# Packing the last tokens of eight experts four to a tile: 34 expert tiles for 39, first weights streamed

## The reference, cut to what matters

```python
xn = layernorm(x)
# attention branch, per token t and head (4 heads of 64)
y_t[i] = sum_j r_t[j] * (S[i,j] + u[j]*k_t[j]*v_t[i]);  S[i,j] = S[i,j]*exp(w_t[j]) + k_t[j]*v_t[i]
attn = (groupnorm(y) * gamma + beta) * g @ Wo.T
# expert branch
probs    = softmax(tokens @ Wr + br)            # 4096 x 8
expert   = argmax(probs);  max_prob = probs[expert]
h        = relu(tokens @ W1[expert] + b1[expert])   # 256 -> 512
ffn      = (h @ W2[expert] + b2[expert]) * max_prob # 512 -> 256
out = x + attn + ffn
```

## Time and profile before

| | |
|---|---|
| median of 3 runs | 571.99 us (569.68 to 573.77) |
| the profiled execution | 572.14 us, span 570.9 us, mean granted TensorE clock 0.988 |
| PE busy | 525.3 us (92% of the span) |
| DVE busy | 440.6 us (77%) |
| ACT busy | 334.5 us (59%) |
| POOL busy | 196.2 us (34%) |
| DMA | 64.03 MB, mean 112 GB/s |
| HBM | read 42.92 MB, written 24.12 MB |

### The profile page before, as it was taken

The page is one execution under the profiler, slowest core; times in us unless marked ns, Lnnn a source line. Parts: engine busy times, 40 slices in busy tenths (PEclk is TensorE's granted clock), DMA queues, the critical chain, the costliest instruction groups (busy, mean ns, idle before and its releaser), DMA issues. The chain is left out here.

```text
span 570.9 us, 20266 instructions
## 1 busy us (share of the span) xinstructions
PE 525.3 (92%) x7946; PEld 465.4 (82%) x7946; DVE 440.6 (77%) x1104; ACT 334.5 (59%) x756; POOL 196.2 (34%) x156
## 2 busy tenths in 40 slices
PE   2889798888999999999999999989999999999984
PEld 2668687776898899989899899979998989989873
DVE  6877899988867696868778886949686877878552
ACT  4964656225574756566665657565655656575751
POOL 7901010121324434334344232533442533523332
PEclk9999999898999999999999999999999999999998
DMA  8978662699431534434333434243443433332334
GB/s 284 305 272 274 183 168 62 158 363 319 108 61 30 111 54 91 75 84 74 90 56 79 78 67 77 49 94 53 95 71 84 70 92 56 66 46 49 48 44 46
DMA packets 57633, 64.03 MB, mean 112 GB/s; under 512 B 10706, under 2 KB 51923, under 8 KB 57395
## 3 DMA queue, kind: packets, MB, share of 16 engines
q1 hardware_dynamic: 44578, 47.77, 29.7%
q0 software_dynamic: 11840, 14.42, 17.3%
q10 hardware_dynamic: 1120, 0.54, 0.3%
HBM read 42.92 MB, written 24.12 MB: 117 GB/s over the span
## 5 line engine op out<-in xcount | busy, mean ns | idle before, releaser
L1802 POOL DMA_INDIRECT out<-rows,dst_row x39 | 64.5, 1654 | 210.1 <-DVE rows L1192 184.7
L704 PE MATMUL F<-xsT,w1s 128*128 128x128 f32 x624 | 76.9, 276 | 2.8 <-issue 1.7
L1064 DVE SCALAR_TENSOR_TENSOR mix<-G,vec,ba 128x256 f32<-128x256 f32 x160 | 69.7, 477 | 12.6 <-PE G L474 12.5
L704 PEld LDWEIGHTS F<-xsT,w1s 128*128 128x128 f32 x624 | 74.6, 192 | 5.5 <-issue 2.5
L712 PE MATMUL F<-w,hsT 128*128 x312 | 74.9, 383 | 0.3 <-ACT hsT L1596 0.3
L1596 ACT ACTIVATE hsT<-F,b1c 128x128 f32<-128x128 f32 x156 | 44.5, 368 | 34.9 <-PE F L704 31.0
L712 PEld LDWEIGHTS F<-w,hsT 128*128 128x128 f32 x312 | 57.2, 190 | 8.5 <-issue 0.5
L1103 DVE COPY_PREDICATED AP_<-msk,LL 128x256 f32<-128x256 uint32 x96 | 51.1, 532 | 16.4 <-issue 11.1
L1125 DVE TENSOR_TENSOR RK<-RK,D 128x256 f32<-128x256 f32 x112 | 47.3, 423 | 19.3 <-issue 11.0
L1072 DVE TENSOR_TENSOR mix<-mix,xnT 128x512 f32<-128x512 f32 x80 | 55.1, 689 | 1.6
L1788 POOL DMA_INDIRECT rows<-xn_d,src_row x39 | 41.0, 1050 | 31.9 <-PE F L693 14.4
(11 more groups left out here) (192 smaller groups left out, 1195.4 us busy)
## 6 DMA issues: line engine op xcount, KB each, us to landing
cd<-cd_d SPq DMA_DIRECT2D x30, 320.0 KB, 5.8
w<-in_W SPq DMA_DIRECT2D x16, 512.0 KB
cd_d<-w SPq DMA_DIRECT2D x32, 160.0 KB, 2.7
b2t<-in_b SPq DMA_DIRECT2D x38, 128.0 KB
w<-in_x SPq DMA_DIRECT2D x8, 512.0 KB, 9.0
xn_d<-w SPq DMA_DIRECT2D x8, 512.0 KB
out<-in_x SPq DMA_DIRECT2D x8, 512.0 KB, 5.4
out<-res POOLq DMA_DIRECT2D x16, 256.0 KB, 4.6
```

Of the source, the lines that this page charges most:

```text
L704: i1 = pe.matmul(FB[:, k * P:(k + 1) * P], w1s[:, cc, k, :], xsT[:, cc, :], start=(cc == 0), stop=(cc == 1))
L1064: i1 = dve.scalar_tensor_tensor(mixed_in(u, c, n, cc), bk[:, cc * UN:(cc + 1) * UN], cvec(LAM + CC * n, cc), ba[:, cc, :, :].rearrange("p ...
L1802: pool.indirect_dma_start(io["out"], bass.IndirectOffsetOnAxis(dst_row[:, f:f + 1], 0), ys[:, f % 2, :], None, compute_op=ALU.add).then_in ...
```

## The change

Tiles are now of two kinds. 25 full tiles hold 128 tokens of one expert each. What is left over of the experts is cut into quarters of 32 tokens, each of one expert, and four quarters make one of 9 quad tiles: 34 tiles for 39. The quads are `fa` of halves 2 to 6 and `fc` of halves 8 to 11. Halves 7 to 13 are now all short (two tiles).

- Full tile: the first weights come from memory by `first_weights` (512 KB) into one of two buffers; ACT's copy `weights` is gone. The rest is as before.
- Quad tile: `hidden` is turned round. The stationary operand is 32 tokens, the moving one 512 columns of the quarter's own W1, and each quarter has its own group of 32 columns of PE (`tile_position=(0, 32*t)`). DVE then adds `b1` (`biased`, 128x512), PE transposes the sum with 4 transposes (`turned`), ACT rectifies with one instruction of 512 columns, and `down` runs 16 matmuls of 256 columns in the four column groups. `quarters` loads four W1, three W2 (the first quarter uses the resident W2) and four `b1` per quad, 11 DMAs; `bias` is four DMAs of 32 partitions.
- W1 is no longer resident; its place holds the quads' weights. W2's load now stands without W1's ahead of it, and the first `first_weights` and `quarters(0)` follow when the experts of the tiles are known (`ex`).
- The routing has 28 numbered steps instead of 16. `tiles_of_experts` is 16 small instructions instead of 5, `places` 4 instead of 1, `experts_of_tiles` 4 instead of 3.
- `rectified(fa)` on ACT stands behind `squares`. For a quad `fc`, `rectified` stands behind `block` and `gated_back`.
- `first_bias`, the gathers, the row sums and all attention code are unchanged; the mask table is stored more tightly.

```diff
-FT = (TOK + E * (P - 1)) // P
-EACH = [0 if h == 0 else 2 if h % 6 == 1 else 3 for h in range(NU - 2)]
+QR = P // 4
+FULL = -(-(TOK - E * (P - 1)) // P)
+QUADS = -(-((TOK - FULL * P + E * (QR - 1)) // QR) // 4)
+FT = FULL + QUADS
+NENTRY = FULL + 4 * QUADS
+EACH = [0 if h == 0 else 3 if 2 <= h <= 6 else 2 for h in range(NU - 2)]
+QUAD = [FIRST[h] for h in range(2, 7)] + [FIRST[h] + 1 for h in range(8, 12)]
...
             def hidden(f):
                 pe.wait_ge(s["fx"], f + 1)
                 if f:
                     pe.wait_ge(s["fy"], f)
-                pe.wait_ge(s["fw"], f + 1)
-                for k in range(HC):
+                if f in QUAD:
+                    pe.wait_ge(s["wq1"], 64 * (quads_to(f) + 1))
                     for cc in range(CC):
-                        i1 = pe.matmul(FB[:, k * P:(k + 1) * P], w1s[:, cc, k, :], xsT[:, cc, :], start=(cc == 0), stop=(cc == 1))
+                        for t in range(4):
+                            at = slice(QR * t, QR * (t + 1))
+                            i1 = pe.matmul(FB[at, 0:HID], xsT[:, cc, at], w1q[:, t, cc, :],
+                                           start=(cc == 0), stop=(cc == 1), tile_position=(0, QR * t))
+                else:
+                    i = fulls_to(f)
+                    pe.wait_ge(s[f"wf{i % 2}"], 16 * (i // 2 + 1))
+                    for k in range(HC):
+                        for cc in range(CC):
+                            i1 = pe.matmul(FB[:, k * P:(k + 1) * P], first_of[i % 2][:, cc, k, :], xsT[:, cc, :], start=(cc == 0), stop=(cc == 1))
                 i1.then_inc(s["fhm"])
+            def turned(f):
+                if f in QUAD:
+                    pe.wait_ge(s["fq"], quads_to(f) + 1)
+                    for k in range(HC):
+                        i1 = pe.transpose(FB[:, k * P:(k + 1) * P], hq[:, k * P:(k + 1) * P], ident)
+                    i1.then_inc(s["fqt"])
 
             def down(f):
...
+                if f in QUAD:
+                    pe.wait_ge(s["wq2"], 48 * (quads_to(f) + 1))
                 for k in range(HC):
-                    i1 = pe.matmul(FB[:, 0:C], hsT[:, k, :], w2[:, bass.ds(number[f] * (HC * C) + k * C, C)], start=(k == 0), stop=(k == HC - 1))
+                    own = w2[:, bass.ds(number[f] * (HC * C) + k * C, C)]
+                    if f in QUAD:
+                        for t in range(4):
+                            at = slice(QR * t, QR * (t + 1))
+                            i1 = pe.matmul(FB[at, 0:C], hsT[:, k, at], w2q[:, t - 1, k, :] if t else own,
+                                           start=(k == 0), stop=(k == HC - 1), tile_position=(0, QR * t))
+                    else:
+                        i1 = pe.matmul(FB[:, 0:C], hsT[:, k, :], own, start=(k == 0), stop=(k == HC - 1))
                 i1.then_inc(s["fym"])
 
             def half(h):
...
                 read_out(u, c, 1)
+                if fa is not None:
+                    turned(fa)
                 decay_up(u, c + 1)
...
                 gated_back(u, c)
+                turned(fc)
                 gate_down(u, c + 1)
...
+            def biased(f):
+                if f in QUAD:
+                    dve.wait_ge(s["fhm"], f + 1)
+                    dve.wait_ge(s["b1q"], 64 * (quads_to(f) + 1))
+                    dve.tensor_tensor(hq[:, :], FB[:, 0:HID], hq[:, :], ALU.add).then_inc(s["fq"])
...
                 added(u, c + 1, 1)
+                if fa is not None:
+                    biased(fa)
                 mixed(u, c + 1, 2)
...
                 gated(u, c)
+                biased(fc)
                 grow(*v, 64)
...
+            def first_weights(i):
+                if i > 1:
+                    sp.wait_ge(s["fhm"], FULLS[i - 2] + 1)
+                e = sp.value_load(expert[0:1, i:i + 1], min_val=0, max_val=E - 1)
+                sp.dma_start(first_of[i % 2].rearrange("p c k n -> p c (k n)"),
+                             io["W1"][bass.ds(e * C, C), :].rearrange("(c p) n -> p c n", p=P)).then_inc(s[f"wf{i % 2}"], 16)
+            def quarters(n):
+                if n:
+                    sp.wait_ge(s["fhm"], QUAD[n - 1] + 1)
+                    sp.wait_ge(s["fqt"], n)
+                    sp.wait_ge(s["fym"], QUAD[n - 1] + 1)
+                for t in range(4):
+                    at = FULL + 4 * n + t
+                    e = sp.value_load(expert[0:1, at:at + 1], min_val=0, max_val=E - 1)
+                    sp.dma_start(w1q[:, t, :, :], io["W1"][bass.ds(e * C, C), :].rearrange("(c p) n -> p c n", p=P)).then_inc(s["wq1"], 16)
+                    if t:
+                        sp.dma_start(w2q[:, t - 1, :, :], io["W2"][bass.ds(e * HID, HID), :].rearrange("(k p) n -> p k n", p=P)).then_inc(s["wq2"], 16)
+                    sp.dma_start(hq[QR * t:QR * (t + 1), :], io["b1"][bass.ds(e * HID, HID)].partition_broadcast(QR)).then_inc(s["b1q"], 16)
 
             def half(h):
...
                 keep_gate(*other(u, c))
-                for f in tiles_of(h):
-                    if f is not None:
-                        bias(f + 1)
-                gate(*other(u, c))
+                own = [f for f in tiles_of(h) if f is not None]
+                for f in own:
+                    if f - 1 in QUAD and quads_to(f) < QUADS:
+                        quarters(quads_to(f))
+                    bias(f + 1)
+                    if f not in QUAD and fulls_to(f) + 2 < FULL:
+                        first_weights(fulls_to(f) + 2)
+                    if f == own[0]:
+                        gate(*other(u, c))
```

More of the change, by code:

```diff
@@ L35, with quads_to, fulls_to, entry @@
 NU = 2 * NCH
-FT = (TOK + E * (P - 1)) // P
-EACH = [0 if h == 0 else 2 if h % 6 == 1 else 3 for h in range(NU - 2)]
+QR = P // 4
[4 more added lines that the diff above has]
+EACH = [0 if h == 0 else 3 if 2 <= h <= 6 else 2 for h in range(NU - 2)]
 FIRST = [sum(EACH[:h]) for h in range(NU - 1)]
 LAST = list(range(FIRST[-1], FT))
+QUAD = [FIRST[h] for h in range(2, 7)] + [FIRST[h] + 1 for h in range(8, 12)]
+assert len(QUAD) == QUADS and len(LAST) == 3
+def quads_to(f):
+    return sum(q < f for q in QUAD)
+def fulls_to(f):
+    return f - quads_to(f)
+def entry(f):
+    return FULL + 4 * quads_to(f) if f in QUAD else fulls_to(f)
+FULLS = [f for f in range(FT) if f not in QUAD]
+def bias_landed(f):
+    return sum(64 if n in QUAD else 16 for n in range(f % 2, f + 1, 2))
 MX, TDM, UU, LAM = [CC * n for n in range(4)]
@@ L950, in vector_program @@
             m1 = small[:, 0:NT]
-            tl, en = small[:, 32:40], small[:, 40:48]
+            flat_of = lgs[:, 0:4 * E]
+            fin, tl, fex, qn = (flat_of[:, E * n:E * (n + 1)] for n in range(4))
+            fboth = flat_of.rearrange("p (k e) -> p k e", e=E)[:, 0:3:2, :]
+            starts = flat_of[:, E:3 * E]
+            qin, c31 = small[:, 32:40], small[:, 40:48]
             rank8 = rout[:, RANK8:RANK8 + NT * E].rearrange("p (t e) -> p t e", e=E)
@@ new lines, in tiles_of_experts @@
+                step(16, dve.tensor_copy(qn, whole[:, :]))
+                step(17, dve.tensor_tensor_scan(qin, qn, qn, 0.0, ALU.add, ALU.bypass))
+                step(18, dve.tensor_tensor(qn, qin, qn, ALU.subtract))
+                step(19, dve.tensor_scalar(starts, starts, float(P), None, ALU.mult))
+                step(20, dve.scalar_tensor_tensor(qn, qn, float(QR), tl, ALU.mult, ALU.subtract))
+                step(21, dve.scalar_tensor_tensor(qn, qn, float(P * FULL), fex, ALU.add, ALU.subtract))
@@ L1629, in half @@
                     rectified(fb)
-                    weights(fb + 1)
                 saved(*v, 16)
@@ L1637, in half @@
                 receptance(u, c + 1)
-                if fc is not None:
+                if fc in QUAD:
+                    block(*v)
+                    gated_back(u, c)
                     rectified(fc)
-                gated_back(u, c)
-                block(*v)
+                else:
+                    rectified(fc)
+                    gated_back(u, c)
+                    block(*v)
                 if h == NU - 3:
@@ L1646, in half @@
                     spread(*v)
-                if fc is not None:
-                    weights(fc + 1)
                 if not short(h + 1):
@@ L1734, in scalar_program @@
             rectified(LAST[0])
-            weights(LAST[1])
             saved(1, c, 16)
@@ L1743, in scalar_program @@
             spread(1, c)
-            weights(LAST[2])
             tokens(LAST[2])
@@ L1979, in sync_program @@
                 sp.dma_start(w2[:, e * HC * C:(e + 1) * HC * C].rearrange("p (c n) -> p c n", c=HC),
-                             io["W2"][e].rearrange("(c p) n -> p c n", p=P)).then_inc(s["ew2"], 16)
+                             io["W2"][e * HID:(e + 1) * HID, :].rearrange("(c p) n -> p c n", p=P)).then_inc(s["ew2"], 16)
+            sp.wait_ge(s["ex"], 1)
+            first_weights(0)
+            first_weights(1)
+            quarters(0)
             for h in range(1, NU - 2):
@@ L1984, in sync_program @@
```

(10 more changed lines are left out.)

118 lines of the change are left out of this document (65 added, 53 removed).

## The result

The changed kernel takes 589.14 us (median of 4 runs), the kernel before beside it 570.84: a ratio of 1.031, 95% interval 1.024 to 1.039. The forecast was 565, the range 557 to 580, so the sign was wrong too. Executions come in two states, a faster and a slower one, and the ratios are of the faster runs alone, so they can differ a little from the quotient of two medians. The profiled execution of the changed kernel takes 587.83 us (span 586.5); that of before took 572.14.

What follows compares the result with a forecast made beforehand. PE was taken to bound the main loop, DVE the prologue. 572.1 - 15.1 (halves 7 to 12) + 1.5 (half 8's gap) + 3.2 (quads) + 2.0 (routing) + 1.5 (late bias) = 565.2 us; range 557 to 580.

Steps and rivals of the forecast that it cites:

- I take 0.3 per half, +1.5: Halves 2 to 6: `bias(fc)`, queued behind `quarters`, lands just in time for ACT's `last_bias(fc)`; 0.3 us per half, +1.5 in all.
- the burst at 321 GB/s: Halves 2 to 6: rate left for a quad's loads beside other traffic; 4.06 MB take 12.6 us.
- the 1.5 for landing: Halves 2 to 6: 1.5 us added to the burst's 12.6 for landing, so the bias is there at 24.6.
- the deadline of 25.8: Halves 2 to 6: latest the bias may land, about 25.8 us into the half, before PE's `output` is late.
- The burst is late: Rival at ACT's `last_bias(fc)`, halves 2 to 6: 230 GB/s costs 19.5 us in place of 1.5, making 583; chance 0.15.
- My bound of 3.9 per half: Halves 2 to 6: upper bound on the late bias's cost at 230 GB/s, 3.9 us per half.
- I count 0 for these three: Fourth W1 in halves 9 to 11, POOL's sums under load, and `first_weights(0)` at the start: no cost, 0 us.
- Routing, +2.0: Prologue on DVE: extra steps in `tiles_of_experts`, `places` and `experts_of_tiles` cost 2.0 us together, bounds 0 to +4.
- A short half between short ones, 28.1: Halves 7 and 12: PE's length estimated from half 7 with `output` counted once, 28.1 us each.
- DVE takes over: Rival in halves 7 to 12: DVE's order keeps a short half at 29.82, gaining 4.7 against costs of 6.7; 574; chance 0.18.
- Quads, +0.65 on PE: Each quad costs PE 0.65 us over a full tile: +3.2 in halves 2 to 6, 28.75 for each of halves 8 to 11.
- I give it back: +1.5: Half 8: PE's 1.52 us gap inside a group of records, with no wait shown, is not removed by the change; +1.5.

Runs made afterwards that it cites:

- the version with small loads: Changed kernel, same queue order, each of a quad's W1 and W2 loads cut to an eighth of its columns: 568.06 us, ratio 0.994 to the kernel before.
- The shifts: 8, 16, 24 or 32 unused one-column matmuls at PE's start, added to the later first quad version: ratios 1.003, 0.994, 1.001, 1.009.
- later first quad: Changed kernel with b2 issued ahead of the burst and `quarters(0)` moved from SP's prologue into half 1: 577.43 us, ratio 1.005.
- with 16 matmuls: The later first quad version plus 16 unused one-column matmuls in PE's first idle stretch: 570.52 us, ratio 0.994.
- with 32: The later first quad version plus 32 unused one-column matmuls in PE's first idle stretch: 579.67 us, ratio 1.009.
- with 24: The later first quad version plus 24 unused one-column matmuls in PE's first idle stretch: 567.86 us, ratio 1.001.
- the second run: Repeat, on another chip, of the later first quad version plus 16 unused one-column matmuls at PE's start: 569.09 us, ratio 0.997.
- the spread version: Changed kernel with b2 ahead and `quarters` of halves 1 to 6 loaded in three parts (two, one, one) over the half: 582.56 us, ratio 1.014.

## Why the prediction was wrong, step by step

**"I take 0.3 per half, +1.5" for the late b2: the step that failed.** The mechanism, the instruction and the engine were right and written down; the term was mis-sized, by a factor of ten. Halves 2 to 5 take 34.5 where the version with small loads takes 31.6: 2.9 each. The wrong steps are the burst at 321 GB/s and the 1.5 for landing, 14.1 us together. In half 3 it is 17.2 us from the first issue to the landing of the b2, an effective 236 GB/s, and the first issue is at 11.4 and not at 10.5. That makes 28.6, 2.8 later than the deadline of 25.8, and so the 2.9 per half are explained. With 2.9 in each of five halves in place of the 1.5 in all, the forecast would have been 578, slower by 1%.

Where the 3.1 us between 14.1 and 17.2 go is seen in part. In the first 5 us, with SP still at its eleven issues and four reads of an expert number, the core moves only 182 GB/s, and then 337, in which loads issued behind the b2 and other traffic have their part. SP's slow issuing alone is not the loss: with small loads it is as slow, and the b2 is there 24.6 us in. Nor is the 1.5 for landing in any row; with small loads the b2 takes 2.9 from issue to use. The 7.9 that it takes in the changed kernel is the rest of the burst still ahead of it. That the earlier trace rows have 7.9 too, for the row sums under load on another queue, is coincidence.

**The rival.** "The burst is late" was right in place, in mechanism and nearly in size: it has the b2 land 29.7 into the half and 3.9 lost, and measured are 28.6 and 2.9. At 0.15 its chance was too low, since the forecast beside it had hardly a margin. Its sum, 583, is near the 588 in part by luck: halves 2 to 6 are 13.4 over the forecast, with a gap of 3.5 in half 6 among them, and not 18, and the rest comes from half 1 and from gaps. My bound of 3.9 per half held.

**Half 1 and the prologue, "I count 0 for these three".** Wrong for the start: the same queue order, with the first quad's loads ahead of tile 1's b2. PE waits 2.52 us for zT at 159.72, then the clock is at its lower level for `output` and `down`:

```profile
159.72 3.78 PE L716 MATMUL YB<-wo,sq 128*128 128x256 f32 x8 [2.52 <-ACT sq L1649]
163.29 3.18 PE L776 MATMUL F<-w,hsT 128*128 x8
```

The granted clock is 0.52 from 159.72 to 166.13. Half 1 is 3.2 us longer than before. The late b2 costs more than that: with b2 ahead of the quad's loads half 1 takes 31.27, so 5.8 go with it. The other 2.6 are a gain at the start of the half that the forecast didn't have: before, PE waits 2.21 for the mixture and the clock falls behind it (granted 0.84 from 126.11 to 137.00); in the changed kernel it waits 1.1, and the clock stays at 1.00. Half 2 then starts at 158.85 in place of 166.13.

**Routing, +2.0.** Half 1 starts 2.97 later: within the bounds 0 to 4, 1.0 short.

**A short half between short ones, 28.1.** Halves 7 and 12 take 27.98 and 27.87. The rival "DVE takes over" had 29.8 and falls.

**Quads, +0.65 on PE; halves 8 to 11 at 28.75.** Halves 8 and 9 take 28.88 and 28.94. A quad's `hidden` in half 10 and its `down` in half 8, in four column groups:

```profile
417.97 1.92 PE L743 MATMUL F<-w,xsT 128*32 128x512 f32 x16
419.82 0.62 PE L634 MATMUL LL<-RK 64*64 64x64 f32 x14
```
```profile
395.03 1.93 PE L773 MATMUL F<-w,hsT 128*32 x32
396.89 0.50 PE L510 MATMUL G<-cd,bst 128*128 128x256 f32 x2
```

From start to start 1.85 and 1.86, with 6.92 one after the other: 3.7 of 4, as the 3.65 of the earlier trace rows said. The Trainium skill ("TensorE: Matmul & The Clock Gate", "Measured speedup vs the span model") gives 2.38 times for three column groups with 512 columns. Carried to four groups this makes 2.18 us, an estimate, and the measured 1.85 goes against it.

**"I give it back: +1.5" for half 8's gap.** Right in kind, short in size. Gaps put down to "issue" are 9.1 us, 5.2 more than before, and those of halves 6 and 10 bring half clock with them. Of the 5.1 us too many in halves 7 to 12 all is in halves 10 and 11. The shifts show that the gaps are no property of the work: the versions do the same and have them in different places, and their halves 2 to 12 add up to 343.9 (later first quad), 339.7 (with 16 matmuls), 338.4 (with 32) and 338.2 (with 24), where halves without gap or wait would make about 329.

**Why 565 is not reached even in the best versions.** From before to the version with 24 matmuls, halves 2 to 12 shrink from 342.0 to 338.2, and half 2 starts 3.0 later. The halves themselves are what was forecast: without gaps, halves 7 to 12 would take 171.1 (27.95, four of 28.8, 27.85), 15.2 less than before, and halves 2 to 6 five times 31.54, 1.9 more. But 338.2 - 328.8 = 9.4 are given back in gaps and small waits, and the kernel before had fewer of these. The 3.0 are mostly the time of the 24 added matmuls: with 16, in the second run, half 2 starts at 159.08, 0.9 earlier than before, and halves 2 to 12 take 340.3.

**What stays open.** That the gaps are PE's waiting for its own instructions rests on timing, and no run forced it. Read packet by packet, in 34 of the 35 gaps of 1 us and more that all traces here show from half 1 on (waits for "issue"), one packet of the instruction queue (q8, 16 KB) ends 1.3 to 1.7 us before PE goes on; the one left is 1.39 at 183.81 in the kernel before. In the gap before 334.97 shown above it starts at 332.62 and ends at 333.50. The window from 332 to 333:

```profile
q8 instruction: 1, 0.02, 5.5%
```

The page counts 65 such packets over the span, and most have no gap beside them: what makes one of them late stays open. In half 10 it is in part the bytes on the queues, as told above. The share of other traffic, of SP's issuing and of the landing itself in the 3.1 us above wasn't separated. Reading a quad's W2 from the resident copy, which would take 1.6 of the burst's 3.9 MB away, wasn't tried.

## What to carry to other kernels

When a change puts a burst of large loads on a queue, look at every small load issued behind it, and count for its landing all bytes still ahead of it, at the rate from the first issue to the last landing and not at that of the best window; then issue the small one first. Where the margin is small and the rate is a guess, a rival that differs only in the rate deserves more weight. Where PE is busy without a break, a difference of one per cent between two versions can be where its stream has gaps; shift the stream by some dozens of instructions before reading it as a property of the change, and take off what the added instructions cost by themselves.

## What was unexpected of the hardware

Some pauses of PE were followed by several us of work at the lower clock: 3.78 for 1.89 behind the 2.52 of half 1, 3.35 for 1.89 behind the 3.53 of half 6, 3.64 for 1.92 behind the 5.20 of the spread version. In half 1 a wait of 2.52 so cost 5.8. Others were not: behind the 2.70 of half 3 `down` took 1.89 as ever and the half was longer by the wait alone, and behind 2.17 at 382.25 (later first quad) the group took 1.92. The length doesn't tell them apart, since behind 1.65 in half 10 of the changed kernel `down` took 2.92.

Gaps of 1 to 4 us inside a group of like matmuls, with no wait shown, move with 32 to 128 instructions added half a millisecond ahead, and end 1.3 to 1.7 us after a packet of the instruction queue. In sum they don't shrink with the bytes on the queues (9.2 against 9.4 us).

The kernel before alone had medians of 570.8, 572.7, 575.9 and 569.5 us in the four comparisons: only ratios within one of them can be compared.
